# Masks prepared a block earlier and adjacency products behind the edge softmax, in a four-layer graph network kernel

## What is computed

```python
h = x @ W
s = leaky_relu(h @ a_node, 0.2)
alpha = softmax(where(H.T > 0, s, NEG), axis=nodes)      # (b, e, n)
agg = einsum('ben,bnf->bef', alpha, h)
beta = sigmoid((h @ a_gn)[:, None, :] + (agg @ a_ge)[:, :, None])
all_he = elu(beta * h + (1 - beta) * agg)
deg = maximum(adj.sum(-1), 1.0)
industry = einsum('nm,bmf->bnf', adj / deg, x @ W_ind)
se = tanh(elu(agg) @ fcW + fcb) @ av
coefs1 = softmax(where(H > 0, se, NEG), axis=edges)
g = einsum('bne,benf->bnf', coefs1, all_he)
# then a softmax over the pair (industry, g)
```

## Time and profile before

| | |
|---|---|
| median of 3 runs | 3417.58 us (3417.16 to 3417.95) |
| the profiled execution | 3417.75 us, span 3415.7 us |
| TensorE busy | 3089.7 us (90%) |
| VectorE busy | 2989.7 us (88%) |
| ScalarE busy | 2293.5 us (67%) |
| POOL busy | 820.3 us (24%) |
| mean granted TensorE clock | 0.972 of full |

### The profile page before, as it was taken

One profiled execution on the slowest core, in us unless ns is written; L12 is line 12 of the kernel. 1 busy time (PEld: TensorE's weight loads), 2 busy tenths in 40 slices (PEclk: granted clock), 3 DMA queues, 4 the chain that ended last, 5 costly groups with the idle time before them and its releaser, 6 DMA issues. The chain is left out here.

```text
span 3415.7 us, 48269 instructions
## 1 busy us (share of the span) xinstructions
PE 3089.7 (90%) x15547; PEld 1884.4 (55%) x15547; DVE 2989.7 (88%) x3847; ACT 2293.5 (67%) x3481; POOL 820.3 (24%) x572
## 2 busy tenths in 40 slices
PE   7997799999999999999999999799596888888857
PEld 3665566666666666566666666599553333333323
DVE  2477899999999999999999999688738999999944
ACT  0121677777777777777777777677335999999831
POOL 0222000000000000000000000000105999999921
PEclk9998999999999999999999999899798999999978
DMA  3000000000000000000000000000000000000001
GB/s 87 1 1 10 1 1 0 0 0 0 0 0 0 0 0 0 0 0 0 0 0 0 0 0 0 1 1 0 2 7 1 1 1 1 1 1 1 0 2 25
DMA packets 30363, 12.15 MB, mean 4 GB/s; under 512 B 27984, under 2 KB 29264, under 8 KB 30288
## 3 DMA queue, kind: packets, MB, share of 16 engines
q1 hardware_dynamic: 25056, 10.04, 1.3%
q10 hardware_dynamic: 5232, 1.12, 0.2%
HBM read 9.06 MB, written 2.10 MB: 3 GB/s over the span
## 5 line engine op out<-in xcount | busy, mean ns | idle before, releaser
L572 ACT ACTIVATE hid_work<-hid_work,hid_nmax 128x1024 f32<-128x1024 f32 x512 | 589.1, 1151 | 305.0 <-DVE hid_nmax L556 305.0
L544 DVE TENSOR_TENSOR hid_work<-hid_score_ps,A 128x1024 f32<-128x1024 f32 x512 | 619.8, 1211 | 28.4 <-PE hid_score_ps L505 28.4
L556 DVE CUSTOM_DVE_ANT_0 hid_work<-hid_masks,hid_work 128x1024 f32<-128x1024 f32 x512 | 622.0, 1215 | 0.2 <-DVE hid_masks L564 0.2
L1591 POOL TENSOR_TENSOR el<-el,node_edge 128x1024 f32<-128x1024 f32 x256 | 611.2, 2388 | 18.4 <-DVE el L1573 12.7
L583 ACT COPY hid_probsT<-hid_turn_ps 128x512 f32<-128x512 f32 x1024 | 542.5, 580 | 98.7 <-PE hid_turn_ps L519 98.7
L519 PEld LDWEIGHTS hid_turn_ps<-ident,hid_work 128*128 128x128 f32 x4096 | 457.6, 140 | 248.0 <-issue 204.5
L519 PE MATMUL hid_turn_ps<-ident,hid_work 128*128 128x128 f32 x4096 | 544.7, 276 | 5.2 <-ACT hid_probsT L583 3.9
L745 PE MATMUL hid_mix_ps<-hid_probsT,x_now 128*64 128x512 f32 x2048 | 495.9, 604 | 34.0 <-DVE hid_Zn L819 31.1
L504 PE MATMUL hid_score_ps<-hid_SX,hid_Y 128*128 (+1 forms) x1024 | 476.5, 465 | 1.6 <-DVE hid_Yl L937 1.4
L505 PE MATMUL hid_score_ps<-hid_SX,hid_Yl 128*128 (+1 forms) x1024 | 403.3, 394 | 0.0
L1544 PE MATMUL spread<-hT_parts,pick 128*128 128x512 f32 x1024 | 307.5, 423 | 65.2 <-DVE u_buf L1567 62.1
(11 more groups left out here) (270 smaller groups left out, 4066.7 us busy)
## 6 DMA issues: line engine op xcount, KB each, us to landing
A<-in_adj_dram SPq DMA_DIRECT2D x4, 1024.0 KB, 9.7
X<-in_x_dram SPq DMA_DIRECT2D x8, 256.0 KB, 8.6
out_dram<-X SPq DMA_DIRECT2D x8, 256.0 KB, 3.4
wa<-in_L_gnn_weight_dram ACTq DMA_DIRECT2D x2, 256.0 KB, 14.0
wb<-in_L_gnn_weight_dram ACTq DMA_DIRECT2D x2, 256.0 KB, 14.2
wh<-in_L_gnn_Wh_dram SPq DMA_DIRECT2D x2, 256.0 KB, 4.3
incid<-in_L_gnn_H_dram SPq DMA_DIRECT2D x2, 256.0 KB, 3.5
wo<-in_L_gnn_W_out_dram SPq DMA_DIRECT2D x1, 256.0 KB, 5.0
```

The costliest lines, as they stand in the source:

```text
L544: nc.vector.tensor_tensor(work[:, kk % 4, :], score_ps[kk % 2][:], A[:, kk % NT, :], ALU.mult).then_inc(s["weighted"], 1)
L556: nc.vector.tensor_tensor_reduce(work[:, kk % 4, :], masks[:, kk % 2, :], work[:, kk % 4, :], -1.0, 3.0e38, ALU.add, ALU.min, nmax[:, kk % ...
L572: nc.scalar.activation(work[:, kk % 4, :], work[:, kk % 4, :], ACT.Exp, bias=nmax[:, kk % 4:kk % 4 + 1], scale=-1.0, accum_out=rowsum[:, k ...
L1591: nc.gpsimd.tensor_tensor(el[:, q % ELS, :], el[:, q % ELS, :], coefT[:, q // C, :], ALU.mult).then_inc(s_weighted, 1)
```

## The change

- The degrees go from block A to stage 0: one reduction of 128x1024 behind each of VectorE's eight copies, then the maximum and the reciprocal.
- The incidence, the vectors and a_ge are loaded in block A, the incidence ahead of the weights and the rest behind them. TensorE transposes the incidence there, and VectorE makes all masks between its xT copies and its hT copies. The transposes of the adjacency wait for memberT, whose banks they use.
- In block B the scores run two couples ahead (sc has two buffers). Only adjacency product 0 lies in the softmax rounds, in two halves: four matmuls under exp 0, four behind turn 2. The other seven follow the hyperedge part, with the industry units and the turns of the coefficients between them.
- The industry units go to the two small banks. ScalarE takes them in four activations of 128 columns with the reciprocal degree as scale, in place of VectorE.
- The rounding of hT goes from ScalarE to VectorE, behind the last adjacency copy.
- The exp of the cell softmax stand between ScalarE's copies.

```diff
+                    nc.vector.tensor_reduce(rdeg[:, t:t + 1], A[:, t, :], AX.X, ALU.add).then_inc(deg_made, 1)
+                vec.wait_ge(deg_made, NT)
+                nc.vector.tensor_scalar(rdeg[:], rdeg[:], 1.0, None, ALU.max).then_inc(deg_made, 1)
+                vec.wait_ge(deg_made, NT + 1)
+                nc.vector.reciprocal(rdeg[:], rdeg[:]).then_inc(deg_made, 1)
...
         hT_parts = sb("hT_parts", [P, 2, J, N], F32R, l2_scope)
         AxT = coefT
         wi2 = sb("wi2", [P, P], F32, l2_scope)
-        rdeg = sb("rdeg", [P, NT], F32, l2_scope)
         fcw = sb("fcw", [P, P], F32, l2_scope)
         fcb = sb("fcb", [P, 1], F32, l2_scope)
         av = sb("av", [P, 1], F32, l2_scope)
         late_scope = ExitStack()
         hT = sb("hT", [P, J, N], F32, late_scope)
         hN = sb("hN", [P, J, NT, P], F32, late_scope)
+        incid = sb("incid", [P, NT, 2, E], F32, late_scope)
+        member = sb("member", [P, NT, E], F32, late_scope)
+        outside = sb("outside", [P, NT, E], F32, late_scope)
+        memberT = sb("memberT", [P, N], F32, late_scope)
+        outsideT = sb("outsideT", [P, N], F32, late_scope)
+        a_rows = sb("a_rows", [P, 3], F32, late_scope)
+        a_node2 = sb("a_node2", [P, P], F32, late_scope)
+        a_gn2 = sb("a_gn2", [P, P], F32, late_scope)
+        a_ge = sb("a_ge", [P, C], F32, late_scope)
...
+                    sp.dma_start(incid[:, :, half, :], Hn).then_inc(in_loaded, 16)
                 sp.wait_ge(zeroed, 2)
                 for m, w in ((w2, L2_W), (wi2, L2_W_ind)):
                     for part in couple_blocks(m):
...
+                    for half in range(2):
+                        sp.dma_start(a_rows[half * C:(half + 1) * C, k:k + 1], v.unsqueeze(1)).then_inc(a_loaded, 16)
+                sp.dma_start(a_ge[:], L2_a_ge.unsqueeze(0).to_broadcast([P, C])).then_inc(a_loaded, 16)
                 sp.wait_ge(loaded, 16 * 8)
+                sp.wait_ge(in_loaded, 16 * 2)
+                sp.wait_ge(a_loaded, 16 * 5)
 
...
                 nc.gpsimd.memset(wi2[:], 0.0).then_inc(zeroed, 1)
+                nc.gpsimd.memset(a_node2[:], 0.0).then_inc(a_zeroed, 1)
...
+                vec.wait_ge(in_loaded, 16 * 2)
+                vec.wait_ge(a_loaded, 16 * 5)
+                vec.wait_ge(a_zeroed, 2)
+                for m, k in ((a_node2, 0), (a_gn2, 1)):
+                    for half in range(2):
+                        rows = slice(half * C, (half + 1) * C)
+                        nc.vector.tensor_copy(m[rows, rows], a_rows[rows, k:k + 1].to_broadcast([C, C]))
+                for half in range(2):
+                    cols = slice(half * HALF, (half + 1) * HALF)
+                    vec.wait_ge(in_banked, half + 1)
+                    nc.vector.tensor_scalar(memberT[:, cols], banks[half][:], 0.0, None, ALU.is_gt).then_inc(masked, 1)
+                nc.vector.tensor_scalar(member[:], incid[:, :, 0, :], 0.0, None, ALU.is_gt).then_inc(masked, 1)
+                vec.wait_ge(masked, 3)
+                nc.vector.tensor_scalar(outsideT[:], memberT[:], -NEG, NEG, ALU.mult, ALU.add)
+                nc.vector.tensor_scalar(outside[:], member[:], -NEG, NEG, ALU.mult, ALU.add).then_inc(masked, 1)
...
                     last.then_inc(xt_banked, 1)
+                pe.wait_ge(in_loaded, 16 * 2)
+                for half in range(2):
+                    for t in range(4 * half, 4 * half + 4):
+                        last = nc.tensor.transpose(banks[half][:, t % 4 * P:(t % 4 + 1) * P],
+                                                   incid[:, t, :, :].rearrange("p h e -> p (h e)"), ident[:])
+                    last.then_inc(in_banked, 1)
...
-            a_ge = sb("a_ge", [P, C], F32, scope)
-            sc = sb("sc", [P, N], F32, scope)
...
                 def copy_score(j):
                     act.wait_ge(s_made, j + 1)
-                    if j:
-                        act.wait_ge(s_leaked, j)
-                    nc.scalar.copy(sc[:], wide[0][:]).then_inc(s_copied, 1)
+                    if j >= 2:
+                        act.wait_ge(s_leaked, j - 1)
+                    nc.scalar.copy(sc[:, j % 2], wide[0][:]).then_inc(s_copied, 1)
...
                 copy_score(0)
+                copy_score(1)
                 for j in range(J):
 
                     act.wait_ge(s_ht, j + 1)
                     nc.scalar.activation(lk[:, j % 2, :], lk[:, j % 2, :], ACT.Exp, bias=small[:, j:j + 1], scale=-1.0,
                                          accum_out=small[:, 4 + j:5 + j]).then_inc(s_exped, 1)
-                    copy_ax(j + 1)
-                    if j + 1 < J:
-                        copy_score(j + 1)
                     act.wait_ge(s_turned, j + 1)
                     if j:
                         act.wait_ge(s_agg, j)
                     nc.scalar.copy(alphaT[:].rearrange("p t k -> p (t k)"), wide[1][:]).then_inc(s_turn_copied, 1)
...
+                def coef_exp(j):
                     act.wait_ge(s_lowered, j + 1)
                     nc.scalar.activation(cells[:, j], cells[:, j], ACT.Exp).then_inc(s_cexp, 1)
-                    if j == 0:
-                        copy_ax(J + 3)
-                for j in range(J):
-                    nc.scalar.copy(hT_parts[:, 0, j, :], hT[:, j, :]).then_inc(h_rounded, 1)
-                for j in range(J):
+
+                def take_ind(n):
+                    j, cols = units[n]
+                    act.wait_ge(ind_made, n + 1)
+                    for a, t in enumerate(range(cols.start // P, cols.stop // P)):
+                        last = nc.scalar.activation(ind[:, j, t].rearrange("p h f -> p (h f)"),
+                                                    banks[n % 2][:, a * P:(a + 1) * P], ACT.Copy, scale=rdeg[:, t:t + 1])
+                    last.then_inc(ind_taken, 1)
+
+                def copy_coef(j):
                     act.wait_ge(s_ct, j + 1)
                     nc.scalar.copy(coefT[:, j, :], wide[j % 2][:]).then_inc(s_ct_copied, 1)
+
+                copy_ax(0)
+                copy_ax(1)
+                coef_exp(0)
+                for n in range(2, 2 * J):
+                    copy_ax(n)
+                    take_ind(n - 2)
+                    if n - 1 < J:
+                        coef_exp(n - 1)
+                    if n == 6:
+                        copy_coef(0)
+                copy_coef(1)
+                take_ind(2 * J - 2)
+                copy_coef(2)
+                take_ind(2 * J - 1)
+                copy_coef(3)
...
-                for n, (j, cols) in enumerate(units):
-                    tiles = slice(cols.start // P, cols.stop // P)
-                    vec.wait_ge(ind_made, n + 1)
-                    nc.vector.tensor_tensor(ind[:, j, tiles].rearrange("p t h f -> p t (h f)"),
-                                            wide[2][:, cols].rearrange("p (t k) -> p t k", k=P),
-                                            rdeg[:, tiles].unsqueeze(2).to_broadcast([P, NT // 2, P]),
-                                            ALU.mult).then_inc(ind_taken, 1)
+                vec.wait_ge(ax_copied, 2 * J)
+                for j in range(J):
+                    nc.vector.tensor_copy(hT_parts[:, 0, j, :], hT[:, j, :]).then_inc(h_rounded, 1)
                 for j in range(J):
                     vec.wait_ge(h_rounded, j + 1)
                     nc.vector.tensor_tensor(hT_parts[:, 1, j, :], hT[:, j, :], hT_parts[:, 0, j, :],
...
-                def ax(n):
+                def ax(n, part):
 
                     j, cols = units[n]
-                    if n >= 2:
+                    if part == 0 and n >= 2:
                         pe.wait_ge(ax_copied, n - 1)
-                    for mt in range(NT):
+                    for mt in range(4 * part, 4 * part + 4):
                         last = nc.tensor.matmul(wide[2][:, cols], Xj[:, j, mt, :], AT[:, mt, cols],
                                                 start=(mt == 0), stop=(mt == NT - 1))
-                    last.then_inc(ax_made, 1)
-
-                ax(0)
-                pe.wait_ge(loaded, 16 * 7)
-                for t in range(NT):
-                    last = nc.tensor.transpose(wide[0][:, t * P:(t + 1) * P], incid[:, t, :, :].rearrange("p h e -> p (h e)"),
-                                               ident[:])
-                last.then_inc(s_h, 1)
-                pe.wait_ge(v_steps, 10)
+                    if part:
+                        last.then_inc(ax_made, 1)
+
...
+                def industry(n):
+                    j, cols = units[n]
+                    pe.wait_ge(ax_copied, n + 1)
                     if n >= 2:
                         pe.wait_ge(ind_taken, n - 1)
-                    for t in range(cols.start // P, cols.stop // P):
-                        tile = slice(t * P, (t + 1) * P)
-                        last = nc.tensor.matmul(wide[2][:, tile], AxT[:, j, tile], wi2[:], start=True, stop=True)
+                    else:
+                        pe.wait_ge(s_tanh, 1)
```

(74 more changed lines are left out.)

82 lines of the change are left out of this document (12 added, 70 removed).

## The result

The changed kernel takes 3408.56 us (median of 7 runs, 3406.0 to 3409.17) against 3417.58 before: 9.0 us less, a ratio of 0.9971 with a 95% interval of 0.996 to 0.9982. The forecast was 3407.2 with a range of 3401.5 to 3412.5. The profiled execution took 3408.83 us at a span of 3406.8.

The account below looks back on a forecast made before the run. The prediction took block ends to bound the kernel, with TensorE carrying block B around a 16.2 us wait for VectorE. Stage 0 +1.5, block A +6.2 and block B -18.1 sum to -10.4: 3407.2 us, range 3401.5 to 3412.5.

Parts of the forecast that it names:

- Block B, -18.1: Edge softmax block: reordered work removes the 16.2 us wait, VectorE's rounded parts end at 101.8 against 119.9 us.
- The walk from instruction to instruction: Block B: forecast start and end times counted from the block's start, score 0 at 0 to VectorE's end at 101.8 us.
- Rival C: Block B's tail: ScalarE bounds it, an industry unit costing 2.5 us and the tail ending at 105; 3410.4 us, chance 0.08.
- Block A, +6.2: Block A: waiting for a_ge and the masks delays TensorE 4.4 us, and a fall of the clock adds 1.8.
- 4.2 us is longer than both, so I take a fall: Block A: TensorE's wait exceeds earlier gaps of 1.31 and 2.73 us, so the clock falls, costing 1.8 us.
- Stage 0, +1.5: Stage 0: the eighth degree reduction delays the copy TensorE waits for by 1.5 us, bounds 1.3 and 3.3.
- that loss has already been paid there once: Stage 0: the square's 1.8 us clock loss was already there before the change, so none was added to 1.5.
- The rest, 0: Stretches the change does not touch, up to block A and from block 3 to the end: no change in time.
- A's case: Loads early, no clock fall in block A, tight hand-overs: -14.2 us in all, 3403.4 us; chance 0.22.
- B's fall in stage 0: Rival: clock falls in stage 0 and block B's opening, 1.8 us each, block 3 1 us later; 3411.8 us, chance 0.14.
- D: Block B: clock stays low through the long run of adjacency products, 3466 us if for the whole run; chance 0.03.
- E: Block B: adjacency products wait for copies queued behind exp, the 16 us return in pieces; 3419 us at worst, chance 0.03.

Follow-up runs that it names:

- ind_vector: The changed kernel with VectorE taking the industry units again, behind the cell softmax in its list, from the two small banks: 3417.86 us, ratio 0.9996.
- masks_in_b: The changed kernel with incidence, vectors and all mask work back at the beginning of block B, adjacency product 0 whole over the loads: 3414.81 us, ratio 0.9987.
- after_again: The changed kernel measured a second time, nothing altered: 3406.35 us.
- mask_split: The changed kernel with only memberT ahead of the hT copies in block A, the vectors and other masks behind them: 3401.43 us, ratio 0.9954.
- ax_whole: The changed kernel with adjacency product 0 in one piece under exp 0, nothing of it behind turn 2: 3411.39 us, ratio 0.9978.
- after_filled: The changed kernel with 19 idle transposes on TensorE under stage 0's wait for the embedding copy: 3405.24 us, ratio 0.9961.
- both_late: The changed kernel with both the eighth degree reduction moved behind the bias products' copy and the masks split around the hT copies: 3399.83 us, ratio 0.9946.
- deg_last: The changed kernel with the eighth degree reduction, maximum and reciprocal behind VectorE's copy of the bias products (the late reduction): 3402.29 us, ratio 0.9955.

## Why the prediction was right, and where not

The forecast was 10.4 us less, and the measured difference 9.0 on the first set of runs and 11.9 on the second (3418.27 less 3406.35). The mechanism of the large term, block B, was right. That the sum came so close is in part luck: in the profile, stage 0 cost 2.8 us more than forecast, and layer 1, which the change does not touch, happened to be 2 us shorter. Step by step:

- **Block B, -18.1.** Measured -18.5 in the profile, and 101.63 to 101.65 us in all nine profiles that have this block as changed. The walk from instruction to instruction was right to 0.3 us at each point up to the elu products. Two terms were a little off: from those to the edge scores it took 6.28 us, not 5.9, and VectorE's tail 7.05 us, not 7.4. Shown by ind_vector: with the adjacency products over the cell softmax and VectorE still taking the units, 3.8 of the 16.2 us of wait remain and the tail is late, 10.1 us together; ScalarE's taking removes these. Shown by masks_in_b: with the masks in the block, the same new order takes 117.84 us, only 2.3 less than before, and some 8 less if one takes off the 5.7 us of low clock. So neither part has a price of its own: take one away, and more than half of the 18.5 is gone. Rival C (ScalarE bounding the tail) is out: a piece costs less than the 0.309 assumed, and ScalarE ends 0.8 us ahead of VectorE.
- **Block A, +6.2.** Measured +6.5, the sum of two terms that were each off. The wait was 3.7, not 4.4: a_ge was there 12.0 us into the block (forecast 12.2: issued 0.4 earlier than my middle value, at the lower bound, and landed 0.3 later: the four vectors went out at 0.6 us each and were not held up by the incidence, whose own DMAs took 0.5 each in the earlier trace rows, not the 0.6 that I read there), and the masks took 3.54, not 4.0. The low clock cost 2.8 in this profile, not 1.8, but over the seven profiles with this wait (37.35, 37.40, 37.42, 38.75, 39.03, 40.20, 40.32) the block averages 38.6, which is 3.7 of wait and 1.2 of clock. That two errors, -0.7 and +1.0, nearly cancelled here is luck. The step "4.2 us is longer than both, so I take a fall" was too simple: three of seven showed none. The Trainium skill ("TensorE: Matmul & The Clock Gate", Part 1) says that the chip watches activity on a schedule of its own, which does not start with the kernel, so that the place of the change varies. These seven agree in that the same wait, 3.2 to 3.4 us long, was followed by the lower level in four and not in three.
- **Stage 0, +1.5.** The wait was forecast nearly right: TensorE waited 1.25 us more, just under the lower bound of 1.3. But the stretch grew by 4.3, above the upper bound of 3.3, since the step "that loss has already been paid there once" failed. Five more profiles with this code in stage 0 (after_again, mask_split, ind_vector, ax_whole, masks_in_b) have 14.38 to 16.02, and the time without any loss is 12.7 (11.43 + 1.25). So the clock costs 1.7 to 4.7 there with the early reduction. With the late one it cost 0, 3.3 and 3.3, and in the order of before 1.7 and 1.7. Whether the longer hole makes it worse on average, these few profiles can't say; after_filled speaks against it. By medians, the late reduction gained 4.1 us over after_again, on another chip, but 1.6 over mask_split, on the same one, which is little more than the wait. What makes the clock fall here stays open.
- **The rest, 0.** It was -2.3 up to block A and +0.4 at the end, though no instruction there changed. Nearly all of the -2.3 is in layer 1: its long part (from the first `hid_score_ps` product to ScalarE's first copy of V) took 1829.4 to 1829.7 us in five profiles and 1831.0 to 1831.5 in eight, in kernels that are identical there, and the changed kernel's profile is one of the five. The rows at its end show where: two small groups of products, each waited for, run at the lower level in one profile and at the full clock in the other. First the kernel before, then the changed one:

```profile
2158.51 1.99 PE L705 MATMUL hid_misc_ps<-hid_Zn,wh_now 128*128 128x512 f32 x2 [0.87 <-DVE h2T L790]
```

```profile
2163.00 1.10 PE L712 MATMUL hid_misc_ps<-hid_Zn,wh_now 128*128 128x512 f32 x2 [0.87 <-DVE h2T L797]
```

  The next group takes 1.98 against 1.08, which makes 1.8 of the 2.0 us. It is why a stage's gain can be read to 0.1 us in a profile and the sum only to 2 or 3.
- **The rivals.** A's case, no fall of the clock in block A, holds in three of seven profiles, but with the wait of 3.7, not with tighter hand-overs. B's fall in stage 0 came (3.0 us more of low clock than before, not 1.8), in block B's opening it did not. D and E found no support: the clock in block B was 1.00, and no adjacency product waited.

## What to carry to other kernels

Work moved into an earlier block is free only where its own wait is free: put the part that needs the late load behind what others are waiting for, as mask_split does for the 3.7 us of wait, and give the last of a series of hidden instructions (the eighth reduction) a place of its own. Before a long series of products is laid over another engine's work, look for who empties its buffers: ind_vector has the same overlap, and its block B loses 10.1 of the 18.5 us. Both repairs together give 3399.9 us, 0.9944 of the kernel before (0.993 to 0.9957), the best version of this study.

## What was unexpected of the hardware

The granted clock changes between executions of the same code, and it moves the time of unchanged parts. The two profiles of the changed kernel have 17.39 and 16.00 us in stage 0 and 40.20 and 38.75 in block A; block 3 to the end took 803.6 to 808.5 us in kernels that are identical there, and stage 0 of both_late had 14.74 and 14.75 us where deg_last, with the same code, had 11.44. A wait of 3.2 to 3.4 us on TensorE was followed by the lower level in four profiles of seven. A difference of 2 us between two profiles of such a kernel is therefore no evidence, unless it lies in a stretch whose rows show why.
